# A graph network's edge loop: the VectorE instructions given one PSUM input each

## Chip, cores and metric

One NeuronCore of a Trainium2 chip runs the kernel. The metric is the device time of one execution, in microseconds (us); lower is better. The kernel is one launch and works in fp32 except for small 0/1 tables in bf16.

## The reference, cut to what matters

Four layers of message passing over 3125 nodes and 100000 edges with 64 channels. The edges arrive sorted by their target `dst`. Each layer does this, with `e` computed once:

```
msg = relu(h[src] + e) + 1e-7             # 100000 x 64
m = msg * t                               # t: one number per layer
seg_max = segment_max(m, dst)             # per node and channel
ex = exp(m - seg_max[dst])
agg = segment_sum(msg * ex, dst) / segment_sum(ex, dst)
out = h + agg
h' = relu(layernorm(out @ w1 + b1)) @ w2 + b2     # then residual and layernorm between layers
```

What takes the time is the part over edges: the gather `h[src]`, the maximum and the two sums per target.

## The kernel before, in words

**Tiles.** The 100000 edges are cut into two halves, one on partitions 0 to 63 and one on 64 to 127 (a partition is a channel of a half), and each half into 98 chunks of 512 edges. The edge loop therefore has 98 turns per layer and 392 in all; a turn works on tiles of 128 x 512 fp32. Layer 0 is written out (it also computes `e`, and counts the edges of each node); layers 1 to 3 are one loop body that runs three times.

**A turn `c`, engine by engine.** GpSimd (POOL in the rows) issues 8 indirect DMAs (L479). Each reads 128 row numbers from the SBUF table `idx_all` and fetches 128 rows of 64 values from `z_rows` in HBM into one of 7 buffers `zsrc`. GpSimd may run 7 turns ahead; it waits for `x_mm` of turn c-7. TensorE (PE) writes `pR` (a row of 0 or -1e30 that marks where a new target begins, L713), adds `e_in` and the gathered rows into `pX` (L722, L727), and transposes the results of the turn before into `pT` (L738, function `back`). ScalarE (ACT) makes `r = relu(pX)` (L556) and `du[1] = r * t` (L558), copies `pT` out (L568), and takes the exponential of the double tile `du`, 1024 elements wide (L562). VectorE (DVE) makes the running maximum `M` with a scan (L1011), `du[0] = pR + M shifted by one` (L1014), subtracts `M` from both halves of `du` in one instruction (L1016), forms `rex = r * ex[1]` (L1023), and scans the two running sums `S` and `W` (L1025, L1027). The sums decay by `exp(du[0])`, which is 0 at a new target, so the last edge of a target holds its sums. SyncE stores `M`, `S` and `W` to HBM and loads `e_in`.

**What sets the order.** Every engine's program is written by hand, with semaphores. `pX`, `pR` and `pT` have two PSUM banks each, used in turn; 8 banks are all there are. In layer 0 VectorE also builds `hot_hi` and `hot_lo` (L1033, L1035, function `node_one_hots`) in 80 of the 98 turns. They stand behind the two sums. After the 98 turns of a layer comes a tail: the last sums are stored, a seam between the halves is mended, 25 more indirect DMAs (L488) fetch each node's sums, and the small matrices and layer norms over nodes run. GpSimd issues no gather of the next layer before that is done.

The lines that the change touches are `messages` and `exps` on ScalarE, `falls` and `add_edges` on TensorE, and `running_max` and `running_sums` on VectorE:

Of the kernel before, what the change touches and what calls it, by code (L numbers as in the profile page):

```python
# [27 lines left out]
P = 128  # L28
# [25 lines left out]
PRE = 2  # L54
# [8 lines left out]
def program(nc, x, src, dst, attr, enc_w, enc_b, edge_w, edge_b, ln_g, ln_b, w1, b1, g1, bb1, w2, b2, t, out):  # L63
    ctx = ExitStack()
    with ctx:
# [64 lines left out]
        r = two("r", [P, CH])  # L130
        du = two("du", [P, 2, CH])
        ex = two("ex", [P, 2, CH])
        rex = sb("rex", [P, CH])
        M = two("M", [P, CH + 1])
# [116 lines left out]
        r_done = sem("r_done")  # L251
        u_done = sem("u_done")
        m_done = sem("m_done")
        d_done = sem("d_done")
        du_done = sem("du_done")
        ex_done = sem("ex_done")
        rex_done = sem("rex_done")
        sw_done = sem("sw_done")
# [239 lines left out]
        def _(act):  # L498
# [30 lines left out]
            act.sem_inc(r_done, PRE)  # L529
            act.sem_inc(u_done, PRE)  # L530
            act.sem_inc(ex_done, PRE)
            act.sem_inc(back_sb, 2 * PRE)
# [5 lines left out]
            def layer(l, first_layer=False):  # L538
# [13 lines left out]
                def messages(c):  # L552
                    s = c % 2
                    act.wait_ge(x_mm, done(g0 + c))
                    act.wait_ge(rex_done, done(g0 + (c - 2)))
                    act.activation(r[s][:, :], pX[s][:, :], ACT.Relu).then_inc(r_done, 1)  # L556
                    act.wait_ge(r_done, done(g0 + c))
                    act.activation(du[s][:, 1, :], r[s][:, :], ACT.Copy, scale=t_now[:, 0:1]).then_inc(u_done, 1)  # L558

                def exps(c):  # L560
                    act.wait_ge(du_done, done(g0 + c))
                    act.activation(ex[c % 2][:, :, :], du[c % 2][:, :, :], ACT.Exp).then_inc(ex_done, 1)  # L562

# [81 lines left out]
        def _(pe):  # L645
# [45 lines left out]
            def layer(l, first_layer=False):  # L691
# [18 lines left out]
                def falls(c):  # L710
                    pe.wait_ge(d_done, done(g0 + (c - 2)))
                    for h in range(2):
                        pe.matmul(pR[c % 2][h * H:(h + 1) * H, :], chunk_sel[:, c:c + 1].to_broadcast([NCH, H]), fall_sb[:, h, :],  # L713
                                  start=True, stop=True)

                def add_edges(c):
                    if first_layer:
                        pe.wait_ge(e_ready, c + 1)
                    else:
                        pe.wait_ge(e_loaded[c % RING], value(pe, (l - 1) * (16 * USES)) + 16 * (c // RING + 1))  # L720
                    pe.wait_ge(r_done, done(g0 + (c - 2)))
                    pe.matmul(pX[c % 2][:, :], ident[:, :], e_in[c % RING][:, :], start=True, stop=False, skip_group_check=True)  # L722
# [114 lines left out]
        def _(dve):  # L837
# [141 lines left out]
            dve.wait_ge(par_in, 16 * N_PAR)  # L979
            for counter in (m_done, d_done, du_done, rex_done, sw_done, agg_done, y_hat_done, hres_done):  # L980
                dve.sem_inc(counter, PRE)
# [10 lines left out]
            def layer(l, first_layer=False):  # L992
# [14 lines left out]
                def running_max(c):  # L1007
                    s, s1 = c % 2, (c - 1) % 2
                    dve.wait_ge(u_done, done(g0 + c))
                    dve.wait_ge(m_stored[s], q0 * 16 + (c // 2 + 1) * 16)  # L1010
                    v.tensor_tensor_scan(M[s][:, 1:CH + 1], pR[s][:, :], du[s][:, 1, :], M[s1][:, CH:CH + 1], ALU.add, ALU.max)  # L1011
                    v.tensor_copy(M[s][:, 0:1], M[s1][:, CH:CH + 1]).then_inc(m_done, 1)
                    dve.wait_ge(m_done, done(g0 + c))
                    v.tensor_tensor(du[s][:, 0, :], pR[s][:, :], M[s][:, 0:CH], ALU.add).then_inc(d_done, 1)  # L1014
                    dve.wait_ge(d_done, done(g0 + c))
                    v.tensor_tensor(du[s][:, :, :], du[s][:, :, :], M[s][:, None, 1:CH + 1].to_broadcast([P, 2, CH]),  # L1016
                                    ALU.subtract).then_inc(du_done, 1)

                def running_sums(c):
                    s, s1 = c % 2, (c - 1) % 2  # L1020
                    dve.wait_ge(ex_done, done(g0 + c))
                    dve.wait_ge(sw_done, done(g0 + (c - 1)))
                    v.tensor_tensor(rex[:, :], r[s][:, :], ex[s][:, 1, :], ALU.mult).then_inc(rex_done, 1)  # L1023
                    dve.wait_ge(back_tp, 2 * g0 + 2 * c + (2 * PRE - 2))
                    v.tensor_tensor_scan(S[s][:, :], ex[s][:, 0, :], ex[s][:, 1, :], S[s1][:, CH - 1:CH], ALU.mult, ALU.add)  # L1025
                    dve.wait_ge(rex_done, done(g0 + c))
                    v.tensor_tensor_scan(W[s][:, :], ex[s][:, 0, :], rex[:, :], W[s1][:, CH - 1:CH], ALU.mult, ALU.add).then_inc(sw_done, 1)  # L1027

# [53 lines left out]
                for c in range(NCH):  # L1082
                    running_max(c)
                    running_sums(c)
                    if first_layer and 0 <= c - HOT_AT < NHB:
                        node_one_hots(c - HOT_AT)
                    if first_layer and c - HOT_AT == NHB + 1:
                        node_ends_1()
# [112 lines left out]
```

## Time and profile before

| | |
|---|---|
| median of 3 runs | 4679.84 us (4676.88 to 4680.34) |
| the profiled execution's own time | 4680.27 us |
| its span, first to last instruction | 4678.2 us |
| GpSimd busy | 3372.7 us (72%) |
| VectorE busy | 2830.4 us (61%) |
| TensorE busy | 2485.0 us (53%) |
| ScalarE busy | 1559.0 us (33%) |
| granted TensorE clock, mean | 0.694 of full |

A busy time is the sum of an engine's instruction durations. GpSimd's spans are the time from taking up a gather to having issued it; the data land later. The gap between two gathers (about 0.30 us) is not counted as busy and is called "issue" in the rows: the engine waited for nothing that the profile shows.

### The profile page before, as it was taken

The numbers are of one execution on the slowest core, as the hardware profiler recorded it, in microseconds if no ns is written. First come the engines' busy times: TensorE is split into PE (matmuls) and PEld (weight loads), VectorE is DVE, ScalarE is ACT, GpSimd is POOL, SyncE is SP. The second block draws the span as 40 slices with busy tenths as digits, with TensorE's granted clock in tenths as the row PEclk, the third lists the DMA queues.
The fourth block names the chain that finished last, engine by engine and source line by source line (L and its number), as shares of the span: only waits on it lengthen the run. The fifth ranks groups of instructions, "written<-read, shape, count | busy, mean of one in ns | idle before, by whom it ended". The sixth has DMA issues, their size and how long they took to land.

```text
span 4678.2 us, 37695 instructions
## 1 busy us (share of the span) xinstructions
PE 2485.0 (53%) x9917; PEld 1798.9 (38%) x9917; DVE 2830.4 (61%) x3516; ACT 1559.0 (33%) x2689; POOL 3372.7 (72%) x3248
## 2 busy tenths in 40 slices
PE   4666666665455555555355555555544555555553
PEld 3444445443333333333233333333332333333333
DVE  5777777765565555555455555555555555555554
ACT  2444444443333333333233333333332333333333
POOL 4777777775577777777557777777746777777773
PEclk9887887877566666666656666666656666666665
DMA  3444444444144444444224444444423444444441
GB/s 87 129 132 130 131 135 128 132 128 127 51 112 112 112 112 112 112 112 112 79 69 113 110 112 111 112 112 111 114 56 89 111 111 112 111 111 111 111 112 48
DMA packets 419935, 506.67 MB, mean 108 GB/s; under 512 B 189115, under 2 KB 190247, under 8 KB 419700
## 3 DMA queue, kind: packets, MB, share of 16 engines
q1 hardware_dynamic: 308294, 393.85, 26.5%
q0 software_dynamic: 108352, 109.48, 12.7%
q8 instruction: 87, 1.43, 0.1%
q14 instruction: 148, 1.21, 0.1%
q10 hardware_dynamic: 3054, 0.71, 0.1%
HBM read 216.21 MB, written 287.39 MB: 108 GB/s over the span
## 4 chain that ended last, share of the span: by engine, by line
POOL 53%; issue 17%; DMA 2%; DVE 2%; PE 1%; ACT 0%; POOLq 0%; DVEq 0%; SPq 0%
POOL zsrc L479 51%; POOL node_sw L488 2%; DMA z_rows<-z 1%; DMA sw_rows<-seam_sw 0%; DMA node_sw<-sw_rows,row_idx 0%; PE pX L796 0%; DVE z L1150 0%; PE pR L817 0%; DVE rden L1121 0%; POOLq L475 0%; ACT sq L601 0%; DMA zsrc<-z_rows,idx_all 0%; PE pT L808 0%; DVE z L1153 0%; DMA seam_sw<-sw_rows 0%
## 5 line engine op out<-in xcount | busy, mean ns | idle before, releaser
L479 POOL DMA_INDIRECT zsrc<-z_rows,idx_all x3136 | 3249.8, 1036 | 1108.9 <-issue 1021.0
L727 PE MATMUL pX<-ident,zsrc 128*128 128x128 f32 x3136 | 790.1, 431 | 1914.7 <-DMA zsrc<-z_rows,idx_all 1914.7
L727 PEld LDWEIGHTS pX<-ident,zsrc 128*128 128x128 f32 x3136 | 675.5, 318 | 2288.6 <-DMA zsrc<-z_rows,idx_all 2287.5
L1011 DVE TENSOR_TENSOR_SCAN M<-pR,M,du 128x512 f32<-128x512 f32 x392 | 503.5, 1284 | 1167.3 <-ACT du L558 1167.3
L556 ACT ACTIVATE r<-pX 128x512 f32<-128x512 f32 x392 | 234.2, 598 | 1986.4 <-PE pX L727 1986.4
L562 ACT ACTIVATE ex<-du 128x1024 f32<-128x1024 f32 x392 | 414.0, 1056 | 777.3 <-DVE du L1016 776.6
L738 PE MATMUL pT<-ident,S 128*128 128x128 f32 x1568 | 638.5, 410 | 30.0 <-DVE W L1027 30.0
L738 PE MATMUL pT<-ident,W 128*128 128x128 f32 x1568 | 628.3, 404 | 0.0
L1023 DVE TENSOR_TENSOR rex<-r,ex 128x512 f32<-128x512 f32 x392 | 281.5, 718 | 440.7 <-ACT ex L562 440.7
L722 PE MATMUL pX<-e_in,ident 128*128 128x512 f32 x784 | 519.5, 749 | 7.5 <-ACT e_in L550 7.5
L1025 DVE TENSOR_TENSOR_SCAN S<-ex,S 128x512 f32<-128x512 f32 x392 | 499.1, 1273 | 0.0
L1027 DVE TENSOR_TENSOR_SCAN W<-ex,W,rex 128x512 f32<-128x512 f32 x392 | 492.0, 1255 | 0.0
L1016 DVE TENSOR_TENSOR du<-du,M 128x1024 f32<-128x1024 f32 x392 | 480.3, 1225 | 13.3
L568 ACT ACTIVATE sw_out<-pT 128x512 f32<-128x512 f32 x784 | 426.7, 586 | 29.4 <-PE pT L738 28.5
L738 PEld LDWEIGHTS pT<-ident,S 128*128 128x128 f32 x1568 | 358.5, 229 | 31.8 <-issue 23.2
L738 PEld LDWEIGHTS pT<-ident,W 128*128 128x128 f32 x1568 | 357.6, 228 | 0.0
L558 ACT ACTIVATE du<-r,t_now 128x512 f32<-128x512 f32 x392 | 283.0, 722 | 12.9
L1014 DVE TENSOR_TENSOR du<-pR,M 128x512 f32<-128x512 f32 x392 | 270.9, 691 | 13.5
L488 POOL DMA_INDIRECT node_sw<-sw_rows,row_idx x100 | 121.2, 1212 | 157.4 <-DMA sw_rows<-seam_sw 94.9
L713 PE MATMUL pR<-fall_sb,chunk_sel 98*64 98x512 bf16 x784 | 203.1, 515 | 15.6 <-DVEq L1171 15.6
L722 PEld LDWEIGHTS pX<-e_in,ident 128*128 128x128 f32 x784 | 145.1, 232 | 137.5 <-issue 106.8
L708 PE MATMUL pA<-attr_t,edge_w 128*128 128x512 f32 x196 | 125.0, 725 | 11.7 <-ACT attr_t L544 11.3
(155 smaller groups left out, 1406.5 us busy)
## 6 DMA issues: line engine op xcount, KB each, us to landing
sw_rows<-sw_out SPq DMA_DIRECT2D x784, 256.0 KB, 2.8
e_in<-e_cols SPq DMA_DIRECT2D x300, 256.0 KB, 2.7
zsrc<-z_rows,idx_all POOLq DMA_INDIRECT x3136
max_cols<-M SPq DMA_DIRECT2D x392, 128.0 KB, 2.3
attr_in<-in_edge_attr_dram SPq DMA_DIRECT2D x196, 128.0 KB
e_cols<-e_in SPq DMA_DIRECT2D x98, 256.0 KB, 2.1
z_rows<-z SPq DMA_DIRECT2D x5, 781.2 KB
node_sw<-sw_rows,row_idx POOLq DMA_INDIRECT x100, 3.3
```

The lines of the kernel that those rows point to most:

```text
L479: pool.indirect_dma_start(zsrc[c % RING][:, t4, h, :], None, z_rows, bass.IndirectOffsetOnAxis(idx_all[:, h, t4, c:c + 1].bitcast(U32), 0) ...
L558: act.activation(du[s][:, 1, :], r[s][:, :], ACT.Copy, scale=t_now[:, 0:1]).then_inc(u_done, 1)
L562: act.activation(ex[c % 2][:, :, :], du[c % 2][:, :, :], ACT.Exp).then_inc(ex_done, 1)
L568: act.activation(sw_out[c % 2][:, :, 2 * b:2 * b + 2, :, :].rearrange("p h t s c -> p (t s) h c"), pT[b][:, :].rearrange("p (a h c) -> p a ...
L722: pe.matmul(pX[c % 2][:, :], ident[:, :], e_in[c % RING][:, :], start=True, stop=False, skip_group_check=True)
L727: last = pe.matmul(pX[c % 2][:, t4:CH:SUB], zsrc[c % RING][:, t4, :, :].rearrange("p h c -> p (h c)"), ident[:, :], start=False, stop=(t4 ...
L738: last = pe.transpose(pT[b][:, at:at + P], scanned[c % 2][:, t4:CH:SUB], ident[:, :])
L1011: v.tensor_tensor_scan(M[s][:, 1:CH + 1], pR[s][:, :], du[s][:, 1, :], M[s1][:, CH:CH + 1], ALU.add, ALU.max)
L1016: v.tensor_tensor(du[s][:, :, :], du[s][:, :, :], M[s][:, None, 1:CH + 1].to_broadcast([P, 2, CH]), ALU.subtract).then_inc(du_done, 1)
L1023: v.tensor_tensor(rex[:, :], r[s][:, :], ex[s][:, 1, :], ALU.mult).then_inc(rex_done, 1)
L1025: v.tensor_tensor_scan(S[s][:, :], ex[s][:, 0, :], ex[s][:, 1, :], S[s1][:, CH - 1:CH], ALU.mult, ALU.add)
L1027: v.tensor_tensor_scan(W[s][:, :], ex[s][:, 0, :], rex[:, :], W[s1][:, CH - 1:CH], ALU.mult, ALU.add).then_inc(sw_done, 1)
```

## The change

Every two-tensor instruction of VectorE in the edge loop now takes one input from PSUM. For that:

- the double tiles `du` and `ex` and the tile `rex` are gone; `u` (r * t) and `decay` are single tiles in SBUF;
- ScalarE writes `r * t` twice, once to `u` in SBUF and once back into `pX` in PSUM;
- VectorE adds `M` to `pR` in place, subtracts `M` from `pR` in place and from `pX` in place: three instructions of 512 elements where there were one of 512 and one of 1024;
- ScalarE's exponential is two instructions of 512: `pR` to `decay`, and `pX` in place;
- `S` is scanned from `decay` and `pX`; then `r` is multiplied into `pX` in place, and `W` is scanned from `decay` and `pX`. The product now comes behind the scan of `S`;
- TensorE may write `pR` again when `decay` is done (was: when the first sum was), and `pX` when `W` is done (was: when `r` was);
- the copy of one column of `M` goes ahead of the scan; in layer 0 `node_one_hots` stands between the maximum and the sums.

```diff
-        du = two("du", [P, 2, CH])
-        ex = two("ex", [P, 2, CH])
-        rex = sb("rex", [P, CH])
+        u = two("u", [P, CH])
+        decay = two("decay", [P, CH])
...
-                    act.activation(du[s][:, 1, :], r[s][:, :], ACT.Copy, scale=t_now[:, 0:1]).then_inc(u_done, 1)
+                    act.activation(u[s][:, :], r[s][:, :], ACT.Copy, scale=t_now[:, 0:1]).then_inc(u_done, 1)
+                    act.activation(pX[s][:, :], r[s][:, :], ACT.Copy, scale=t_now[:, 0:1]).then_inc(u_ps_done, 1)
 
                 def exps(c):
-                    act.wait_ge(du_done, done(g0 + c))
-                    act.activation(ex[c % 2][:, :, :], du[c % 2][:, :, :], ACT.Exp).then_inc(ex_done, 1)
+                    act.wait_ge(dm_done, done(g0 + c))
+                    act.activation(decay[c % 2][:, :], pR[c % 2][:, :], ACT.Exp).then_inc(decay_done, 1)
+                    act.wait_ge(um_done, done(g0 + c))
+                    act.activation(pX[c % 2][:, :], pX[c % 2][:, :], ACT.Exp).then_inc(ex_done, 1)
...
                 def falls(c):
-                    pe.wait_ge(d_done, done(g0 + (c - 2)))
+                    pe.wait_ge(decay_done, done(g0 + (c - 2)))
...
-                    pe.wait_ge(r_done, done(g0 + (c - 2)))
+                    pe.wait_ge(sw_done, done(g0 + (c - 2)))
                     pe.matmul(pX[c % 2][:, :], ident[:, :], e_in[c % RING][:, :], start=True, stop=False, skip_group_check=True)
...
                     s, s1 = c % 2, (c - 1) % 2
+                    v.tensor_copy(M[s][:, 0:1], M[s1][:, CH:CH + 1])
                     dve.wait_ge(u_done, done(g0 + c))
                     dve.wait_ge(m_stored[s], q0 * 16 + (c // 2 + 1) * 16)
-                    v.tensor_tensor_scan(M[s][:, 1:CH + 1], pR[s][:, :], du[s][:, 1, :], M[s1][:, CH:CH + 1], ALU.add, ALU.max)
-                    v.tensor_copy(M[s][:, 0:1], M[s1][:, CH:CH + 1]).then_inc(m_done, 1)
+                    v.tensor_tensor_scan(M[s][:, 1:CH + 1], pR[s][:, :], u[s][:, :], M[s1][:, CH:CH + 1], ALU.add, ALU.max).then_inc(m_done, 1)
                     dve.wait_ge(m_done, done(g0 + c))
-                    v.tensor_tensor(du[s][:, 0, :], pR[s][:, :], M[s][:, 0:CH], ALU.add).then_inc(d_done, 1)
+                    v.tensor_tensor(pR[s][:, :], pR[s][:, :], M[s][:, 0:CH], ALU.add).then_inc(d_done, 1)
                     dve.wait_ge(d_done, done(g0 + c))
-                    v.tensor_tensor(du[s][:, :, :], du[s][:, :, :], M[s][:, None, 1:CH + 1].to_broadcast([P, 2, CH]),
-                                    ALU.subtract).then_inc(du_done, 1)
+                    v.tensor_tensor(pR[s][:, :], pR[s][:, :], M[s][:, 1:CH + 1], ALU.subtract).then_inc(dm_done, 1)
+                    dve.wait_ge(u_ps_done, done(g0 + c))
+                    v.tensor_tensor(pX[s][:, :], pX[s][:, :], M[s][:, 1:CH + 1], ALU.subtract).then_inc(um_done, 1)
 
                 def running_sums(c):
                     s, s1 = c % 2, (c - 1) % 2
+                    dve.wait_ge(decay_done, done(g0 + c))
                     dve.wait_ge(ex_done, done(g0 + c))
                     dve.wait_ge(sw_done, done(g0 + (c - 1)))
-                    v.tensor_tensor(rex[:, :], r[s][:, :], ex[s][:, 1, :], ALU.mult).then_inc(rex_done, 1)
                     dve.wait_ge(back_tp, 2 * g0 + 2 * c + (2 * PRE - 2))
-                    v.tensor_tensor_scan(S[s][:, :], ex[s][:, 0, :], ex[s][:, 1, :], S[s1][:, CH - 1:CH], ALU.mult, ALU.add)
+                    v.tensor_tensor_scan(S[s][:, :], decay[s][:, :], pX[s][:, :], S[s1][:, CH - 1:CH], ALU.mult, ALU.add).then_inc(s_done, 1)
+                    dve.wait_ge(s_done, done(g0 + c))
+                    v.tensor_tensor(pX[s][:, :], r[s][:, :], pX[s][:, :], ALU.mult).then_inc(rex_done, 1)
                     dve.wait_ge(rex_done, done(g0 + c))
-                    v.tensor_tensor_scan(W[s][:, :], ex[s][:, 0, :], rex[:, :], W[s1][:, CH - 1:CH], ALU.mult, ALU.add).then_inc(sw_done, 1)
+                    v.tensor_tensor_scan(W[s][:, :], decay[s][:, :], pX[s][:, :], W[s1][:, CH - 1:CH], ALU.mult, ALU.add).then_inc(sw_done, 1)
...
                 for c in range(NCH):
                     running_max(c)
-                    running_sums(c)
                     if first_layer and 0 <= c - HOT_AT < NHB:
                         node_one_hots(c - HOT_AT)
+                    running_sums(c)
```

VectorE in layer 0, one turn of the stretch with one-hots, before (digits are the buffer of a pair; a scan is listed as SCALAR_TENSOR_TENSOR):

```order
L1011 SCALAR_TENSOR_TENSOR M0<-pR0,M1,du0 128x512 [waits m_stored0,u_done]
L1012 COPY M0<-M1 128x1
L1014 TENSOR_TENSOR du0<-pR0,M0 128x512 [waits m_done]
L1016 TENSOR_TENSOR du0<-du0,M0 128x1024 [waits d_done]
L1023 TENSOR_TENSOR rex<-r0,ex0 128x512 [waits sw_done,ex_done]
L1025 SCALAR_TENSOR_TENSOR S0<-ex0,S1 128x512 [waits back_tp]
L1027 SCALAR_TENSOR_TENSOR W0<-ex0,W1,rex 128x512 [waits rex_done]
L1033 TENSOR_TENSOR hot_hi0<-count_b,hi_b 125x1250 [waits hot_used]
L1035 TENSOR_TENSOR hot_lo0<-count_b,lo_b 125x250
```

and with the change (line numbers are those of the changed kernel):

```order
L1017 COPY M0<-M1 128x1
L1020 SCALAR_TENSOR_TENSOR M0<-pR0,M1,u0 128x512 [waits m_stored0,u_done]
L1022 TENSOR_TENSOR pR0<-pR0,M0 128x512 [waits m_done]
L1024 TENSOR_TENSOR pR0<-pR0,M0 128x512 [waits d_done]
L1026 TENSOR_TENSOR pX0<-pX0,M0 128x512 [waits u_ps_done]
L1044 TENSOR_TENSOR hot_hi0<-count_b,hi_b 125x1250 [waits hot_used]
L1046 TENSOR_TENSOR hot_lo0<-count_b,lo_b 125x250
L1034 SCALAR_TENSOR_TENSOR S0<-decay0,S1,pX0 128x512 [waits sw_done,back_tp,ex_done,decay_done]
L1036 TENSOR_TENSOR pX0<-r0,pX0 128x512 [waits s_done]
L1038 SCALAR_TENSOR_TENSOR W0<-decay0,W1,pX0 128x512 [waits rex_done]
```

The one-hots moved from behind `W` to between the last subtraction and `S`, the product from before `S` to behind it, and one more instruction is issued per turn.

ScalarE in the loop of layers 1 to 3, one turn, before:

```order
L556 ACTIVATE r0<-pX0 128x512 [waits rex_done,x_mm]
L558 ACTIVATE du0<-r0,t_now 128x512 [waits r_done]
L567 REGISTER_ALU [waits sw_stored1]
L568 ACTIVATE sw_out1<-pT0 128x4x2x64 [waits back_tp]
L567 REGISTER_ALU
L568 ACTIVATE sw_out1<-pT1 128x4x2x64 [waits back_tp]
L562 ACTIVATE ex0<-du0 128x1024 [waits du_done]
```

and with the change:

```order
L561 ACTIVATE r0<-pX0 128x512 [waits rex_done,x_mm]
L563 ACTIVATE u0<-r0,t_now 128x512 [waits r_done]
L564 ACTIVATE pX0<-r0,t_now 128x512
L575 REGISTER_ALU [waits sw_stored1]
L576 ACTIVATE sw_out1<-pT0 128x4x2x64 [waits back_tp]
L575 REGISTER_ALU
L576 ACTIVATE sw_out1<-pT1 128x4x2x64 [waits back_tp]
L568 ACTIVATE decay0<-pR0 128x512 [waits dm_done]
L570 ACTIVATE pX0<-pX0 128x512 [waits um_done]
```

Two more instructions per turn: the second `r * t`, ahead of the copies out, and the exponential in two pieces.

## Rows read from the trace of the kernel before

**Rows 1.** The page, the chain that ended last: shares by engine, then by line.

```profile
POOL 53%; issue 17%; DMA 2%; DVE 2%; PE 1%; ACT 0%; POOLq 0%; DVEq 0%; SPq 0%
```

**Rows 2.** GpSimd's gathers: duration in ns, least, median and greatest.

```profile
L479 POOL DMA_INDIRECT zsrc<-z_rows,idx_all x3136: 940/944/2181, 58.8 to 4569.5; - x196
```

**Rows 3.** Busy time of the gathers alone, by stretch: layers 0, 1, 2, 3.

```profile
58.00:1143.00 1085.00, 844.64 (x784) 0.80 0.47 129
1244.00:2282.00 1038.00, 798.35 (x784) 0.68 0.41 111
2384.00:3424.00 1040.00, 800.98 (x784) 0.67 0.40 110
3526.00:4571.00 1045.00, 805.03 (x784) 0.67 0.40 110
```

**Rows 4.** Timeline in layer 2, VectorE and GpSimd: start, duration, instruction, idle before.

```profile
2803.29 1.28 DVE L1011 TENSOR_TENSOR_SCAN M<-pR,M,du 128x512 f32<-128x512 f32 x1 [2.97 <-ACT du L558]
...
2803.95 0.94 POOL L479 DMA_INDIRECT zsrc<-z_rows,idx_all  x1 [0.30 <-issue]
...
2804.65 0.69 DVE L1014 TENSOR_TENSOR du<-pR,M 128x512 f32<-128x512 f32 x1
...
2808.37 1.27 DVE L1025 TENSOR_TENSOR_SCAN S<-ex,S 128x512 f32<-128x512 f32 x1
2808.98 1.42 POOL L479 DMA_INDIRECT zsrc<-z_rows,idx_all  x1 [0.30 <-issue]
2809.57 1.25 DVE L1027 TENSOR_TENSOR_SCAN W<-ex,W,rex 128x512 f32<-128x512 f32 x1
...
2810.70 0.94 POOL L479 DMA_INDIRECT zsrc<-z_rows,idx_all  x1 [0.30 <-issue]
```

**Rows 5.** Timeline in layer 0, the 1024-element subtraction and the one-hots beside gathers.

```profile
701.95 1.45 DVE L1033 TENSOR_TENSOR hot_hi<-count_b,hi_b 125x1250 bf16<-125x1250 bf16 x1
...
703.16 1.06 POOL L479 DMA_INDIRECT zsrc<-z_rows,idx_all  x1 [0.30 <-issue]
703.33 0.41 DVE L1035 TENSOR_TENSOR hot_lo<-count_b,lo_b 125x250 bf16<-125x250 bf16 x1
...
705.47 1.28 DVE L1011 TENSOR_TENSOR_SCAN M<-pR,M,du 128x512 f32<-128x512 f32 x1 [1.73 <-ACT du L558]
...
718.68 1.22 DVE L1016 TENSOR_TENSOR du<-du,M 128x1024 f32<-128x1024 f32 x1
...
719.23 1.49 POOL L479 DMA_INDIRECT zsrc<-z_rows,idx_all  x1 [0.30 <-issue]
```

**Rows 6.** The page's costliest groups: count, busy us, mean ns, idle before and its releaser.

```profile
L479 POOL DMA_INDIRECT zsrc<-z_rows,idx_all x3136 | 3249.8, 1036 | 1108.9 <-issue 1021.0
L727 PE MATMUL pX<-ident,zsrc 128*128 128x128 f32 x3136 | 790.1, 431 | 1914.7 <-DMA zsrc<-z_rows,idx_all 1914.7
...
L1011 DVE TENSOR_TENSOR_SCAN M<-pR,M,du 128x512 f32<-128x512 f32 x392 | 503.5, 1284 | 1167.3 <-ACT du L558 1167.3
L556 ACT ACTIVATE r<-pX 128x512 f32<-128x512 f32 x392 | 234.2, 598 | 1986.4 <-PE pX L727 1986.4
L562 ACT ACTIVATE ex<-du 128x1024 f32<-128x1024 f32 x392 | 414.0, 1056 | 777.3 <-DVE du L1016 776.6
...
L1023 DVE TENSOR_TENSOR rex<-r,ex 128x512 f32<-128x512 f32 x392 | 281.5, 718 | 440.7 <-ACT ex L562 440.7
...
L1016 DVE TENSOR_TENSOR du<-du,M 128x1024 f32<-128x1024 f32 x392 | 480.3, 1225 | 13.3
L568 ACT ACTIVATE sw_out<-pT 128x512 f32<-128x512 f32 x784 | 426.7, 586 | 29.4 <-PE pT L738 28.5
...
L558 ACT ACTIVATE du<-r,t_now 128x512 f32<-128x512 f32 x392 | 283.0, 722 | 12.9
L1014 DVE TENSOR_TENSOR du<-pR,M 128x512 f32<-128x512 f32 x392 | 270.9, 691 | 13.5
```

More of the change, by code:

```diff
@@ L252, in program @@
         u_done = sem("u_done")
+        u_ps_done = sem("u_ps_done")
         m_done = sem("m_done")
         d_done = sem("d_done")
-        du_done = sem("du_done")
+        dm_done = sem("dm_done")
+        um_done = sem("um_done")
+        decay_done = sem("decay_done")
         ex_done = sem("ex_done")
+        s_done = sem("s_done")
         rex_done = sem("rex_done")
@@ L530, in _ @@
             act.sem_inc(u_done, PRE)
+            act.sem_inc(u_ps_done, PRE)
+            act.sem_inc(decay_done, PRE)
             act.sem_inc(ex_done, PRE)
@@ L979, in _ @@
             dve.wait_ge(par_in, 16 * N_PAR)
-            for counter in (m_done, d_done, du_done, rex_done, sw_done, agg_done, y_hat_done, hres_done):
+            for counter in (m_done, d_done, dm_done, um_done, s_done, rex_done, sw_done, agg_done, y_hat_done, hres_done):
                 dve.sem_inc(counter, PRE)
```

## The prediction

> **What bounds the kernel now.** I read the chain of waits first. More than half of the span on it is GpSimd, and 17% is "issue", the pauses between its gathers [rows 1]. The groups say what the rest does meanwhile: TensorE waits 1914.7 us for gathered rows, ScalarE 1986.4 us for TensorE, VectorE 1167.3 us for ScalarE [rows 6]. So inside the edge loop everybody waits for the gathers, and GpSimd waits for nobody: each gather follows the last after 0.30 us [rows 4]. A turn of the loop costs 8 gathers.
>
> Then I asked whether a gather always takes the same time. It does not. The median is 944 ns and the least 940, but the mean is 1036 and the greatest 2181 [rows 2, 6]. Most gathers sit at the floor, and some are held up. What the long ones have in common is seen in the timeline, by laying GpSimd's rows beside VectorE's:
> - A gather that starts 0.66 us into the scan of M takes 0.94 us. That scan reads pR in PSUM and du in SBUF [rows 4].
> - A gather that starts 0.61 us into the scan of S takes 1.42 us. That scan reads two tiles in SBUF. The gather's remaining 0.94 us begin at 2809.46, 0.18 us before the scan is over at 2809.64 [rows 4].
> - A gather that starts 0.55 us into the 1024-element subtraction, again two inputs in SBUF, takes 1.49 us. Its last 0.94 us begin at 719.78, 0.12 us before the end at 719.90 [rows 5].
> - A gather at 703.16 beside hot_hi, also two inputs in SBUF, takes 1.06 us, and its last 0.94 us begin 0.12 us before the end of hot_hi [rows 5].
> - A gather that starts 1.13 us into the scan of W, when under 0.12 us of it is left, takes 0.94 us [rows 4].
>
> So a gather that wants to start while VectorE runs an instruction with two SBUF inputs waits until about 0.12 to 0.18 us before its end, and one with a PSUM input holds up nothing. The gather reads its row numbers from SBUF (idx_all), which is why I take it to be a matter of reading SBUF.
>
> **How much is lost to it.** Per layer the busy time of the 784 gathers less 784 x 0.944 us (740.1 us) is 104.5 us in layer 0, and 58.3, 60.9 and 64.9 us in layers 1 to 3 [rows 2, 3]. The sum is 288.6 us, all of it on the path. This is the most that the change can give by this route.
>
> **The change, part by part.**
>
> *Layers 1 to 3.* Subtraction, product and both scans all get a PSUM input, so no two-input SBUF instruction is left in the loop. The 184.1 us go.
>
> *Layer 0.* The same goes for its loop, but hot_hi and hot_lo still read two SBUF tiles, 80 times. Now each costs 0.12 us at 703.16 [rows 5], some 10 us in all. That is luck of phase: a gather starts 1.21 us into it. With the one-hots moved, they fall elsewhere against the gathers. hot_hi holds gathers up for 1.45 - 0.12 = 1.33 us and a gather starts every 0.944 + 0.30 = 1.244 us, so one always falls inside it. It waits nothing at best and 1.33 us at worst; over evenly spread phases the mean is 1.33 x 1.33 / 2 / 1.244 = 0.71 us. hot_lo adds 0.29 x 0.29 / 2 / 1.244 = 0.03 us. I take the mean, since in layer 0 the landings jitter: 80 x 0.74 = 60 us stay. Bounds 0 and 106 us.
>
> *Longer or shorter VectorE.* Its turn now runs from the start of the M scan to the end of W, 2803.29 to 2810.82, 7.53 us [rows 4]. Afterwards: M scan 1.28 and 0.04 to the next; addition 0.69 + 0.04; first subtraction 0.69; second 0.69, less 0.06 overlap; then it waits for the second exponential, 0.60 with two hand-overs of 0.03; scan S 1.28 + 0.04; product 0.69 + 0.04; scan W 1.28. Sum 7.36 us. The prices: 691 ns for 512 elements with PSUM in and SBUF out, 1284 for a scan with one PSUM input, 598 for an activation of 512 [rows 6]. No row shows VectorE or ScalarE writing PSUM, or an instruction that reads and writes the same bank; the lower bound is the same 691, since nothing there leaves out work. The upper bound is 1225 ns, the row of twice the elements, as if the bank served read and write in turn; for the exponential 1056 in place of 598 [rows 6]. I take the low ends: same element count, same input. With the high ends the turn is 7.36 + 4 x 0.53 + 0.46 = 9.94 us. GpSimd's is 8 x 1.244 = 9.95 us. So even there VectorE only draws level.
>
> *ScalarE* gets one r * t more (722 ns) and one start-up more in the exponential (2 x 598 - 1056 = 140 ns): 0.598 + 2 x 0.722 + 2 x 0.586 + 2 x 0.598 = 4.4 us of a turn of 9.95 [rows 6]. Zero; hidden under the wait for TensorE. The second r * t ends while VectorE is in its M scan, so nobody waits for it. Layer 0 adds two activations of about that size and still has room.
>
> *The two later releases.* TensorE may write pX of turn c+1 only when W of turn c-1 is done. But its program puts the transposes of turn c-1 right ahead, and those wait for the same W. Nothing is queued longer. The same holds for pR and decay. Zero.
>
> *The one-hots ahead of the sums* fill the wait for the exponentials (440.7 us over 392 turns now, 1.12 each [rows 6]). VectorE in layer 0 needs 7.36 - 0.66 + 1.39 + 0.41 = 8.5 us of a turn of about 10.7. Zero.
>
> *Gathers, loads, stores, the tails between layers* are the same instructions in the same order. The time from the last gather to the last sum changes by about 0.2 us in four tails. Zero.
>
> **The sum.** 4680.3 us of the profiled execution (the median of the runs is 4679.8, the same within 0.01%), less 288.6, plus 60: **4452 us**. With the bounds for hot_hi, 4392 to 4498.
>
> **Rivals.**
>
> *A: only the input's place matters, and the wrong one stays.* In the row that shows no hold-up, PSUM is the first input. In the new S, product and W it is the second. If a first input from SBUF holds gathers as well, the subtraction's part goes but the scan's 0.48 us per turn stays [rows 4]: 392 x 0.48 = 188 us. 4452 + 188 = 4640 us. For it: no row has this operand order. Against: both orders need one SBUF read. Chance 0.05.
>
> *B: the hold-up is not VectorE's reading.* Then nothing changes but phases: 4680 us, within a few us. By what mechanism: a gather must write what it issues, and two-input instructions would then not be what stops it. Against it: the end of the wait follows the end of three different instructions with two SBUF inputs within 0.12 to 0.18 us, and never that of the M scan. Chance 0.03. The Trainium skill, "SBUF — State Buffer", section "Who interferes with whom", speaks for B in part: it says that `tensor_tensor` did not stall such DMAs in a probe, and infers that it takes only the shared read interface while the issuing of descriptors needs the write interface. By that the sum would be 4680. The same section also says that two SBUF inputs contend with a GpSimd instruction that reads SBUF. The trace agrees with this second rule and not with the first: 1.49 us beside a `tensor_tensor` [rows 5].
>
> *C: VectorE becomes the bound, slower than before.* The place is the in-place instructions on pR and pX. One turn now takes 1038 / 98 = 10.6 us in layers 1 to 3 [rows 3]. With the exponential at its 1.06 us, VectorE's turn passes 10.6 us if each of the four in-place ones takes over (10.6 - 7.36 - 0.46) / 4 + 0.69 = 1.39 us. That is the point from which it decides. If they cost three times per element (0.16 + 3 x 0.53 = 1.76 us, from 691 and 1225), and the exponential 1.51, the turn is 7.36 + 4.28 + 0.91 = 12.6 us: +2.0 x 294 in layers 1 to 3, and about +1.7 x 80 in layer 0, some 5400 us. For it: no row covers such an instruction. Against: it must be worse than doubled. Chance 0.03.
>
> *D: between.* Doubled prices put VectorE level with GpSimd; then every jitter of a landing is paid by both and the turn is some 0.1 to 0.2 us longer than 9.95: 4452 + 392 x 0.15 = 4510 us. Chance 0.07.
>
> **The numbers.** My forecast has 0.82, A 0.05, B 0.03, C 0.03, D 0.07. A measurement of this kernel tells 0.2% (9 us) from no change. Faster: forecast, A and D, 0.94. Same: B, 0.03. Slower: C, 0.03. The range takes in the forecast's bounds, 4392 to 4498, trimmed at the bottom because no hold-up at all is an unlikely phase, and D at the top: 4400 to 4525.
>
> **What would show it.** The gathers' mean falls from 1036 to about 963 ns (944 + 60 us / 3136), with a median of 944 again. In layers 1 to 3 the 784 gathers take 740 us busy and the stretch 975 instead of 1038. In layer 0 about 800 us, every long gather beside hot_hi or hot_lo. The in-place instructions read 0.69 us, scans 1.28. TensorE still waits for zsrc. The forecast is wrong if gathers of 1.4 us stand beside the new scans (A), if the mean stays at 1036 (B), or if gaps of over 0.30 us appear between gathers in mid-loop because x_mm is late (C, D).

## The result, and the profile after

The changed kernel takes 4442.67 us (median of 4 runs, 4438.64 to 4442.86), the kernel before 4678.36 us. The ratio is 0.9492, 95% interval 0.9481 to 0.9504: **faster by 5.1%**, 236 us. The forecast was 4452 us, in a range of 4400 to 4525. Left out of all that follows are one of the four executions of hot_psum (5396.28 us, the other three 4390.20 to 4391.09) and the first runs of pad_psum3 and hot_psum_behind, beside which the kernel before took 5231.89 us instead of some 4678.

The gathers of the changed kernel, by instruction (duration in ns: least, median, greatest) and by stretch, layers 0 to 3 (busy time of the gathers alone):

```profile
L482 POOL DMA_INDIRECT zsrc<-z_rows,idx_all x3136: 940/944/2232, 58.6 to 4332.1; - x196
```
```profile
58.00:1093.00 1035.00, 792.17 (x784) 0.83 0.48 136
1192.00:2172.00 980.00, 739.94 (x784) 0.68 0.43 117
2273.00:3253.00 980.00, 739.96 (x784) 0.69 0.43 117
3353.00:4334.00 981.00, 740.00 (x784) 0.69 0.43 117
```

Compare [rows 2] and [rows 3]. The least and the median have not moved (940, 944), but in layers 1 to 3 the 784 gathers of a layer now take 740 us, which is 784 x 0.944: none is held up by more than 0.04 us. Layer 0 went from 844.6 to 792.2 us and keeps 52 us above 784 x 0.944.

The page's chain of waits and its groups, the counterparts of [rows 1] and [rows 6]:

```profile
POOL 52%; issue 18%; DMA 2%; DVE 2%; PE 1%; ACT 0%; POOLq 0%; DVEq 0%; SPq 0%
```
```profile
L482 POOL DMA_INDIRECT zsrc<-z_rows,idx_all x3136 | 3012.1, 960 | 1108.4 <-issue 1019.8
L735 PE MATMUL pX<-ident,zsrc 128*128 128x128 f32 x3136 | 772.8, 424 | 1649.7 <-DMA zsrc<-z_rows,idx_all 1649.7
...
L1020 DVE TENSOR_TENSOR_SCAN M<-pR,M,u 128x512 f32<-128x512 f32 x392 | 503.2, 1284 | 1001.2 <-ACT u L563 1000.8
...
L1034 DVE TENSOR_TENSOR_SCAN S<-decay,S,pX 128x512 f32<-128x512 f32 x392 | 500.9, 1278 | 253.2 <-ACT decay L568 240.0
...
L1038 DVE TENSOR_TENSOR_SCAN W<-decay,W,pX 128x512 f32<-128x512 f32 x392 | 501.8, 1280 | 13.8
...
L1022 DVE TENSOR_TENSOR pR<-pR,M 128x512 f32<-128x512 f32 x392 | 274.2, 699 | 13.6
L1024 DVE TENSOR_TENSOR pR<-pR,M 128x512 f32<-128x512 f32 x392 | 274.1, 699 | 13.5
L1036 DVE TENSOR_TENSOR pX<-r,pX 128x512 f32<-128x512 f32 x392 | 272.7, 696 | 13.5
L1026 DVE TENSOR_TENSOR pX<-pX,M 128x512 f32<-128x512 f32 x392 | 269.9, 688 | 0.0
L564 ACT ACTIVATE pX<-r,t_now 128x512 f32<-128x512 f32 x392 | 263.2, 671 | 0.0
...
L570 ACT ACTIVATE pX<-pX 128x512 f32<-128x512 f32 x392 | 228.8, 584 | 0.2
```

The gathers' busy time fell by 3249.8 - 3012.1 = 237.7 us, and the span by 4678.2 - 4441.0 = 237.2 us. That is the whole effect: VectorE is busier than before (2918.6 us against 2830.4), ScalarE too (1819.6 against 1559.0), and both still wait for the gathers. In-place work in PSUM costs what the same shape cost with an SBUF output: 688 to 699 ns against 691; the activations that write PSUM are even a little shorter (671 and 584 ns against 722 for `u` and 595 for `decay`, L563 and L568).

The timeline of one turn in layer 2, VectorE and GpSimd (start, duration, instruction, idle before), the counterpart of [rows 4]:

```profile
2798.42 1.28 DVE L1020 TENSOR_TENSOR_SCAN M<-pR,M,u 128x512 f32<-128x512 f32 x1 [2.76 <-ACT u L563]
...
2802.56 1.28 DVE L1034 TENSOR_TENSOR_SCAN S<-decay,S,pX 128x512 f32<-128x512 f32 x1 [0.79 <-ACT decay L568]
2803.28 0.94 POOL L482 DMA_INDIRECT zsrc<-z_rows,idx_all  x1 [0.30 <-issue]
...
2804.60 1.28 DVE L1038 TENSOR_TENSOR_SCAN W<-decay,W,pX 128x512 f32<-128x512 f32 x1
```

A gather that starts 0.72 us into the scan of S takes 0.94 us, where one at 0.61 us took 1.42 before. Over the whole trace 246 gathers start inside the scan of S (its last 0.21 us aside) and none is held; before the change 302 did, and all 302 were held. VectorE's turn is 2798.42 to 2805.88, 7.46 us. And in layer 0, the one-hots, the counterpart of [rows 5]:

```profile
701.94 1.45 DVE L1044 TENSOR_TENSOR hot_hi<-count_b,hi_b 125x1250 bf16<-125x1250 bf16 x1
...
702.42 1.79 POOL L482 DMA_INDIRECT zsrc<-z_rows,idx_all  x1 [0.30 <-issue]
```

This gather starts 0.48 us into hot_hi and waits 0.85 us, where the one at 703.16 waited 0.12. Of the 52 us left in layer 0, the waits beside hot_hi are 50.7.

### The profile page after: what moved, and what is told of

Same layout as the page of the kernel before. It is cut to its first block, busy times and chain, and to the rows that moved or that the text cites. A ratio compares the mean times of both kernels' runs of the same rounds, so it can differ in the third digit from the quotient of the medians.

```text
span 4441.0 us, 38976 instructions
## 1 busy us (share of the span) xinstructions
PE 2474.3 (56%) x9917; PEld 1760.4 (40%) x9917; DVE 2918.6 (66%) x3908; ACT 1819.6 (41%) x3473; POOL 3135.1 (71%) x3248
## 4 chain that ended last, share of the span: by engine, by line
POOL 52%; issue 18%; DMA 2%; DVE 2%; PE 1%; ACT 0%; POOLq 0%; DVEq 0%; SPq 0%
POOL zsrc L482 50%; POOL node_sw L491 2%; DMA z_rows<-z 1%; DMA sw_rows<-seam_sw 1%; DMA node_sw<-sw_rows,row_idx 0%; PE pX L804 0%; DVE z L1161 0%; DVE rden L1132 0%; PE pR L825 0%; POOLq L478 0%; PE pT L816 0%; ACT sq L609 0%; DMA zsrc<-z_rows,idx_all 0%; DMA seam_sw<-sw_rows 0%; DVE z L1164 0%
## 5 line engine op out<-in xcount | busy, mean ns | idle before, releaser
L482 POOL DMA_INDIRECT zsrc<-z_rows,idx_all x3136 | 3012.1, 960 | 1108.4 <-issue 1019.8
L1020 DVE TENSOR_TENSOR_SCAN M<-pR,M,u 128x512 f32<-128x512 f32 x392 | 503.2, 1284 | 1001.2 <-ACT u L563 1000.8
L1034 DVE TENSOR_TENSOR_SCAN S<-decay,S,pX 128x512 f32<-128x512 f32 x392 | 500.9, 1278 | 253.2 <-ACT decay L568 240.0
L746 PE MATMUL pT<-ident,S 128*128 128x128 f32 x1568 | 629.5, 405 | 51.7 <-DVE W L1038 51.5
L1038 DVE TENSOR_TENSOR_SCAN W<-decay,W,pX 128x512 f32<-128x512 f32 x392 | 501.8, 1280 | 13.8
L568 ACT ACTIVATE decay<-pR 128x512 f32<-128x512 f32 x392 | 233.3, 595 | 379.0 <-DVE pR L1024 379.0
L563 ACT ACTIVATE u<-r,t_now 128x512 f32<-128x512 f32 x392 | 283.0, 722 | 12.9
L1022 DVE TENSOR_TENSOR pR<-pR,M 128x512 f32<-128x512 f32 x392 | 274.2, 699 | 13.6
L1024 DVE TENSOR_TENSOR pR<-pR,M 128x512 f32<-128x512 f32 x392 | 274.1, 699 | 13.5
L1036 DVE TENSOR_TENSOR pX<-r,pX 128x512 f32<-128x512 f32 x392 | 272.7, 696 | 13.5
L1026 DVE TENSOR_TENSOR pX<-pX,M 128x512 f32<-128x512 f32 x392 | 269.9, 688 | 0.0
L564 ACT ACTIVATE pX<-r,t_now 128x512 f32<-128x512 f32 x392 | 263.2, 671 | 0.0
```

Of the source, the lines that this page charges most:

```text
L482: pool.indirect_dma_start(zsrc[c % RING][:, t4, h, :], None, z_rows, bass.IndirectOffsetOnAxis(idx_all[:, h, t4, c:c + 1].bitcast(U32), 0) ...
L563: act.activation(u[s][:, :], r[s][:, :], ACT.Copy, scale=t_now[:, 0:1]).then_inc(u_done, 1)
L746: last = pe.transpose(pT[b][:, at:at + P], scanned[c % 2][:, t4:CH:SUB], ident[:, :])
L1020: v.tensor_tensor_scan(M[s][:, 1:CH + 1], pR[s][:, :], u[s][:, :], M[s1][:, CH:CH + 1], ALU.add, ALU.max).then_inc(m_done, 1)
L1022: v.tensor_tensor(pR[s][:, :], pR[s][:, :], M[s][:, 0:CH], ALU.add).then_inc(d_done, 1)
L1024: v.tensor_tensor(pR[s][:, :], pR[s][:, :], M[s][:, 1:CH + 1], ALU.subtract).then_inc(dm_done, 1)
```

## The experiments

Two theories were open after the result. *The first:* a gather is held up by VectorE's second read from SBUF, wherever it comes from, and GpSimd sets the pace, so the time is a constant plus the held time (what the gathers take beyond 0.944 us each). *The second:* something else about the rewritten loop gave the gain: other lengths, other waits, other phases, or a write. Every edit is made to the changed kernel. The kernel before ran beside each (medians 4676 to 4681 us). A run has 2 to 8 executions, within 10 us of each other. Where the text says how many gathers were held, or sums the waits beside one instruction, that is counted over the whole trace: a wait belongs to the VectorE instruction near whose end it ended.

### A delay of the scan, and the same delay with its input in SBUF

```diff
+        exs = two("exs", [P, CH])
...
+                    act.activation(exs[c % 2][:, :], pX[c % 2][:, :], ACT.Exp)
                     act.activation(pX[c % 2][:, :], pX[c % 2][:, :], ACT.Exp).then_inc(ex_done, 1)
```

> The changed kernel, with one more ScalarE instruction per turn: the exponential of pX is also written to an SBUF tile exs (nobody reads it), ahead of the one in place. S starts some 0.6 us later per turn. It is the control of s_sbuf_late. Theory (a gather is held up only by a VectorE instruction with two SBUF inputs; GpSimd sets the pace): no gather is held in layers 1 to 3, VectorE's turn grows from 7.4 to about 8.0 us of 9.98, time 4443 us within 10. Rival (VectorE's or ScalarE's chain is near to being the bound, so that a delay of 0.6 us per turn shows): 4443 + 392 x 0.6 = 4680 us.

Measured: 4441.65 us. The scan of S waits 1.30 us for the exponentials where it waited 0.79, and that costs nothing; the rival's 4680 is out. Now the same instructions, one operand changed:

```diff
-                    v.tensor_tensor_scan(S[s][:, :], decay[s][:, :], pX[s][:, :], S[s1][:, CH - 1:CH], ALU.mult, ALU.add).then_inc(s_done, 1)
+                    v.tensor_tensor_scan(S[s][:, :], decay[s][:, :], exs[s][:, :], S[s1][:, CH - 1:CH], ALU.mult, ALU.add).then_inc(s_done, 1)
```

> As s_psum_late, instruction for instruction, but the scan of S reads exs in SBUF in place of pX in PSUM, so it has two SBUF inputs. Same values. Theory: each gather that starts in the first 1.1 us of that scan waits until about 0.18 us before its end. By the phases of the changed kernel's timeline, shifted by 0.6 us, the wait is 0.7 to 1.0 us per turn in layers 1 to 3 and 0.5 on average in layer 0: 4443 + 205 to 290 + 47 = 4695 to 4780 us. Rival (the hold-up was not VectorE's second SBUF read but the write side or something else about the old loop): 4443 us, as the control.

Measured: 4553.96 us, 112 us more than the control. In the control 376 gathers start inside the scan of S (its last 0.21 us aside) and none is held; here 298 do and 278 are held, and 19 of the 20 others start in its first 0.1 us. So the mechanism is right and the size was missed: I had expected 250 to 340. The timeline (layer 2, start and duration) shows one reason. One turn has a held gather, the next has none:

```profile
2799.97 1.28 DVE L1036 TENSOR_TENSOR_SCAN S<-decay,S,exs 128x512 f32<-128x512 f32 x1 [1.30 <-issue]
2800.55 1.46 POOL L483 DMA_INDIRECT zsrc<-z_rows,idx_all  x1 [0.31 <-issue]
...
2809.80 0.94 POOL L483 DMA_INDIRECT zsrc<-z_rows,idx_all  x1 [0.30 <-issue]
2809.90 1.28 DVE L1036 TENSOR_TENSOR_SCAN S<-decay,S,exs 128x512 f32<-128x512 f32 x1 [1.30 <-issue]
2811.05 0.94 POOL L483 DMA_INDIRECT zsrc<-z_rows,idx_all  x1 [0.30 <-issue]
```

The second scan falls between two starts: one gather starts 0.10 us ahead of it and is free, the next 1.15 us into it and is free again. What a gather needs to be let in for is its start. The hold is 1.1 us, the gathers' distance 1.25, so a scan can slip through; I had taken one timeline's phase for all turns. In layers 1 to 3 a gather is held in 60 to 65 of a layer's 98 turns, and its wait is 0.45 us on average, where I had 0.7 to 1.0 us in every turn.

### One part undone: the subtraction in SBUF

```diff
-                    v.tensor_tensor(pR[s][:, :], pR[s][:, :], M[s][:, 1:CH + 1], ALU.subtract).then_inc(dm_done, 1)
-                    dve.wait_ge(u_ps_done, done(g0 + c))
-                    v.tensor_tensor(pX[s][:, :], pX[s][:, :], M[s][:, 1:CH + 1], ALU.subtract).then_inc(um_done, 1)
+                    v.tensor_tensor(du[s][:, :, :], du[s][:, :, :], M[s][:, None, 1:CH + 1].to_broadcast([P, 2, CH]),
+                                    ALU.subtract).then_inc(dm_done, 1)
...
```

The cut lines are what this needs: ScalarE writes `r * t` once, to `du`, the addition writes to `du`, and the exponentials read `du`.

> The changed kernel with the subtraction as it was: one instruction of 1024 elements with two SBUF inputs (du, M); the exponentials then go to decay in SBUF and to pX in PSUM, and product and scans stay as changed. Same values. It is the change without one of its parts. Theory: gathers are held only beside this instruction. Its hold is 1.1 us; by the phases of the changed kernel's timeline a gather starts 0.3 to 0.7 us into it, so it waits 0.4 to 0.8 us per turn: 4443 + 130 to 235 in layers 1 to 3 + about 48 in layer 0 = 4620 to 4725 us. So undoing one of four parts may give back nearly the whole gain. Rival (the parts add up: in the kernel before this instruction held gathers for 88 us by its own rows): 4530 us.

Measured: 4585.66 us, 143 us above the changed kernel. That is below my interval, which started at 4620, and above the rival's 4530. The gathers' groups say 3155.0 us busy, 143 us over the changed kernel's. Beside the subtraction the gathers wait 174.8 us, where they waited 86.8 us beside the same instruction in the kernel before. In layer 0 part of it was taken back: hot_hi's waits became short again, 18.8 us in all against 50.7 in the changed kernel. Undoing one part of four loses 60% of the gain, so the parts do not add up: what an instruction costs depends on where the others have left the gathers.

### A useless instruction of three kinds

All three stand between the product and the scan of W and have about the same length. The first, with one input from PSUM:

```diff
+                    v.tensor_tensor(pad_o[:, :, :], pX[s][:, None, :].to_broadcast([P, 2, CH]), pad_b[:, None, :].to_broadcast([P, 2, CH]), ALU.add)
```

> The changed kernel with one useless VectorE addition of 1024 elements per turn between the product and the scan of W, its inputs pX (PSUM) and a constant tile in SBUF. Theory: it takes 1.22 us, VectorE's turn grows to 8.6 us in layers 1 to 3, GpSimd still sets the pace and no gather is held by it: 4443 us within 10. Rival (VectorE's length matters): 4443 + 392 x 1.2 = 4910 us.

Measured: 4439.34 us. 1224 ns more of VectorE per turn cost nothing. A gather beside it, in layer 2:

```profile
2799.69 1.22 DVE L1044 TENSOR_TENSOR pad_o<-pX,pad_b 128x1024 f32<-128x1024 f32 x1
2799.99 0.94 POOL L485 DMA_INDIRECT zsrc<-z_rows,idx_all  x1 [0.30 <-issue]
```

With `pad_a`, in SBUF, in place of `pX[s]`:

> As pad_psum, but both inputs of the useless addition are constant tiles in SBUF. Same length, same place. Theory: a gather that starts in its first 1.1 us waits until 0.12 us before its end; in the changed kernel gathers start 0.1 to 0.4 us behind that point in most turns, so 0.7 to 1.0 us of waiting in most turns: 4443 + 200 to 300 + about 48 = 4690 to 4790 us. Rival (it is not the two SBUF inputs): 4443 us as pad_psum.

Measured: 4664.97 us, 226 us more than with the PSUM input; nearly the whole gain of the change is gone. That is a little under the expectation, for the reason above: in layers 1 to 3 the addition holds a gather in 70 to 75 of 98 turns. The row that does it, in layer 2, with a gather that starts at the same 0.30 us into the addition:

```profile
2807.60 1.22 DVE L1044 TENSOR_TENSOR pad_o<-pad_a,pad_b 128x1024 f32<-128x1024 f32 x1
2807.90 1.75 POOL L485 DMA_INDIRECT zsrc<-z_rows,idx_all  x1 [0.30 <-issue]
```

The last 0.94 us of that gather begin at 2808.71, 0.11 us before the end of the addition. With the PSUM input 361 gathers start inside the addition (its last 0.21 us aside) and none is held; with both inputs in SBUF 301 do and 286 are held, and the 15 others start in its first 0.05 us.

The third is a copy of 2048 elements, SBUF to SBUF, one input:

```diff
+                    v.tensor_copy(pad_o[:, :, :], pad_a[:, :, :])
```

> As pad_sbuf, but the useless instruction is a VectorE copy of 2048 fp32 elements from SBUF to SBUF, one input. Theory of the second read alone: one input, nothing is held, 4443 us. Rival (a copy from SBUF to SBUF holds the gathers too, as if it were reading through both ports): it then takes about 1.2 us and costs as pad_sbuf, 4690 to 4790 us.

Measured: 4743.74 us, more than the kernel before (4675.74). So the theory that only a second tensor matters is wrong, and the rival is right: a copy with one input holds gathers too. It moves 2048 elements in 1.23 us, where the addition needs 1.22 us for 1024. Its rows (layer 2) show a second kind of hold:

```profile
2701.75 0.94 POOL L484 DMA_INDIRECT zsrc<-z_rows,idx_all  x1 [0.30 <-issue]
2702.28 1.46 DVE L1042 COPY pad_o<-pad_a 128x2048 f32<-128x2048 f32 x1
2703.00 1.55 POOL L484 DMA_INDIRECT zsrc<-z_rows,idx_all  x1 [0.30 <-issue]
...
2712.34 1.65 POOL L484 DMA_INDIRECT zsrc<-z_rows,idx_all  x1 [0.30 <-issue]
2712.64 1.23 DVE L1042 COPY pad_o<-pad_a 128x2048 f32<-128x2048 f32 x1
```

The gather at 2712.34 started 0.30 us before the copy and was held all the same: it ends at 2713.99, 0.12 us after the copy's end. In the whole traces neither the scan of s_sbuf_late nor the addition of pad_sbuf holds a gather that has started before it; the copy holds every one that started up to 0.51 us before it. And at 2702.28 it is the copy that is held, 1.46 us in place of 1.23, and it came 0.53 us into a gather; the copies that come 0.51 to 0.74 us into one take 1.48 down to 1.25 us. From this I take it that a gather wants something not only at its start but again in its middle, and that the copy excludes that too; what it is, no run shows.

The Trainium skill, "SBUF — State Buffer", section "Who interferes with whom", has these pieces: an exclusive lock on ports that VectorE and GpSimd share, taken by copies in a two-port mode for reading and writing, and by two SBUF inputs for reading only, the later of the two to wait. The trace agrees in that copies and two-input instructions are the ones that hold gathers, and with 1.46 us for a copy that came second. The section also says that whichever starts first has the ports for its whole instruction; there the trace differs, since the gather at 2712.34 started first and was held. Its remark that `tensor_tensor` did not stall such DMAs does not hold for these indirect ones: 210 us of waits beside the addition here.

### How far VectorE can grow

The addition of pad_psum three times per turn.

> As pad_psum, with three such additions of 1024 elements per turn (pX in PSUM and a constant tile in SBUF, each into its own tile). It looks for the point at which VectorE becomes the bound. Theory: VectorE's turn is 7.4 + 3 x 1.2 = 11.0 us in layers 1 to 3 and about 12.1 in layer 0, against 9.98 and 10.5 of GpSimd now. So VectorE sets the pace: 4443 + 1.0 x 294 + 1.6 x 98 = 4890 us, within 40, and gaps of over 0.30 us stand between gathers in mid-loop. Rival (the slack is larger, because part of the chain overlaps with the next turn's gathers): 4443 us.

Measured: 5438.03 us, left out as said with the result. The same kernel again:

> The kernel of pad_psum3 once more. In that run the kernel before took 5232 us beside it instead of 4680, so it says nothing about pace. Same expectation: VectorE's turn is 11.0 us in layers 1 to 3 and 12.1 in layer 0, and sets the pace: 4890 us within 40. Rival (the slack is larger): 4443 us.

Measured: 4856.31 us, within 40 of the 4890 expected. The groups:

```profile
L484 POOL DMA_INDIRECT zsrc<-z_rows,idx_all x3136 | 3028.7, 966 | 1224.9 <-issue 1001.4
L748 PE MATMUL pT<-ident,S 128*128 128x128 f32 x1568 | 676.6, 432 | 1929.3 <-DVE W L1045 1929.3
```

TensorE now waits for W, 1929.3 us, and hardly for the gathers (78.1 us). The timeline has the scan of S at 2002.55 and again at 2013.36, so the turn is 10.81 us, all of it VectorE's but 0.8 for the exponentials. In the changed kernel eight gathers take 8 x (0.944 + 0.304) = 9.98 us and VectorE's turn 7.46, which leaves an estimated 2.5 us of room per turn. One addition of 1.2 fits and three do not; two were not tried.

### The one-hots: their place, and their input

Back behind the sums, nothing else:

> The changed kernel with the one-hots of layer 0 back behind the two sums; nothing else. Theory: hot_hi and hot_lo still hold gathers up, only at another phase; the sum of their waits is anywhere between 10 us (as before the change) and 106 us (80 x 1.33), so the time is 4400 to 4500 us, and layers 1 to 3 don't change. Rival (the place ahead of the sums matters because it covers the wait for the exponentials): VectorE's turn in layer 0 grows by 0.7 us to 9.2, still under 9.98, so this rival needs layer 0 to get longer with VectorE having no idle time left in a turn: 4443 + 80 x 0.7 = 4500 us.

Measured: 4428.84 us, 14 us faster than the changed kernel. The gathers' busy time is 3003.9 against 3012.1 us, so 8 of the 14 us are held time; the rest lies mostly in the tails between the layers. The place that the change gave them is not the better one.

Where they stand in the changed kernel, with the table of counts in unused columns of the PSUM bank `pH`:

```diff
+            v.tensor_copy(pH[0:NP, 256:256 + NP], count_i[:, :])
+            dve.drain()
...
-                    if n >= 2:
-                        dve.wait_ge(hot_used, n - 1)
+                    if n >= 1:
+                        dve.wait_ge(hot_used, n)
...
-                    v.tensor_tensor(hot_hi[n % 2][:, :, :], count_b[:, None, 0:NP].to_broadcast([NP, HB, NP]),
+                    v.tensor_tensor(hot_hi[n % 2][:, :, :], pH[0:NP, None, 256:256 + NP].to_broadcast([NP, HB, NP]),
...
-                    v.tensor_tensor(hot_lo[n % 2][:, :, :], count_b[:, None, 0:NK].to_broadcast([NP, HB, NK]),
+                    v.tensor_tensor(hot_lo[n % 2][:, :, :], pH[0:NP, None, 256:256 + NK].to_broadcast([NP, HB, NK]),
```

> The changed kernel, and the table of counts that both one-hots compare with is read from 125 fp32 columns of the PSUM bank pH instead of from SBUF; the one-hot of turn n waits until the counting matmuls of n-1, which write that bank, are done. Theory: the last held gathers go, 51 us in layer 0, which leaves 4390 to 4400 us. Risk: the new wait pushes VectorE's turn in layer 0 towards 9.8 us and eats some of it (up to 20 us). Rival (only fp32 tiles of the loop matter, or the mixture of a fp32 PSUM and a bf16 SBUF input still holds gathers): 4443 us.

Measured: **4390.79 us, ratio to the kernel before 0.9379 (0.9360 to 0.9398)**, 52 us faster than the changed kernel: the version that beats both. Its gathers, and a gather that starts 0.80 us into hot_hi, in layer 0:

```profile
L482 POOL DMA_INDIRECT zsrc<-z_rows,idx_all x3136 | 2961.7, 944 | 1108.9 <-issue 1020.5
```
```profile
110.54 1.45 DVE L1046 TENSOR_TENSOR hot_hi<-pH,hi_b 125x1250 bf16<-125x1250 f32 x1
111.34 0.94 POOL L482 DMA_INDIRECT zsrc<-z_rows,idx_all  x1 [0.30 <-issue]
```

The mean is the median, 944 ns. In all 80 turns a gather starts inside hot_hi, anywhere from 0.02 to 1.24 us into it, and none is held; in the changed kernel all 80 are. Both changes to the one-hots together:

> As hot_psum, with the one-hots behind the two sums. Theory: with no gather held by the one-hots their place is worth nothing, 4390 us as hot_psum, within 5. Rival (the place in itself, the cover of the wait for the exponentials or the wait for the counting matmuls, is worth something): it differs from hot_psum by 15 us or more, as hot_behind differs from the changed kernel by 14.

Measured: 5358.32 us, left out for the same reason. The same kernel again:

> The kernel of hot_psum_behind once more, for the same reason. Theory: 4390 us within 5, as hot_psum. Rival (the place of the one-hots in itself is worth something): 15 us or more away from it.

Measured: 4390.51 us. With nothing held, the place is worth nothing. So the 8 us of held time in hot_behind came from where the gathers happened to fall; its other 5 us are not explained.

### All runs on one line

Held time is the gathers' busy time less 3136 x 0.944 = 2960.4 us.

| kernel | span, us | held, us | span less held |
|---|---|---|---|
| before | 4678.2 | 289.4 | 4388.8 |
| changed | 4441.0 | 51.7 | 4389.3 |
| s_psum_late | 4440.7 | 53.5 | 4387.2 |
| s_sbuf_late | 4550.1 | 162.8 | 4387.3 |
| sub_sbuf | 4582.4 | 194.6 | 4387.8 |
| pad_psum | 4437.2 | 48.1 | 4389.1 |
| pad_sbuf | 4662.9 | 269.7 | 4393.2 |
| pad_copy | 4741.8 | 352.1 | 4389.7 |
| hot_behind | 4427.6 | 43.5 | 4384.1 |
| hot_psum | 4388.7 | 1.3 | 4387.4 |
| hot_psum_behind2 | 4387.9 | 1.5 | 4386.4 |

Eleven kernels with held times from 1 to 352 us leave the same 4384 to 4393 us. Only pad_psum3_again leaves the line (4854.2 - 68.3 = 4785.9), because there VectorE sets the pace. So the time is a constant plus the held time, as the first theory has it, and other lengths, waits and places are worth at most some 5 us by themselves, which is against the second. That it is the place of an operand which holds a gather is shown by the two pairs that differ in one operand, s_psum_late with s_sbuf_late and pad_psum with pad_sbuf. The first theory is too narrow in one point: pad_copy's copy has one input and holds gathers as well.

## Why the prediction was right

- **The bound and its loss.** Right. 288.6 us were called the most that could be had by this route; hot_psum gains 4678.2 - 4388.7 = 289.5. In the kernel before, the waits beside the scan of S sum to 145.0 us, beside the subtraction to 86.8, beside the product to 39.5 and beside hot_hi to 17.1.
- **Layers 1 to 3: 184.1 us go.** They went: 740 us of gathers in each. A layer's gathers span 979 us (784 x 1.248) and not the 975 forecast, because the pause between two is 0.304 us and not 0.300; the sum did not use the 975.
- **Layer 0: 60 us stay, bounds 0 and 106.** 52 us stayed, almost all of it beside hot_hi. This term is 8 of the 9 us between forecast and measurement. The waits beside hot_hi run from 0.12 to 1.29 us with a mean of 0.63, against the 0.71 of evenly spread phases, so the assumption holds in this kernel. That the number came so close is in part luck: the same 80 instructions cost 17.1 us in the kernel before (the prediction had some 10), 18.8 in sub_sbuf, 41.2 in hot_behind and 68.0 in pad_psum3_again. My expectations for s_sbuf_late and sub_sbuf, built on one turn's phase, were too high.
- **VectorE's turn, 7.36 us.** Measured 7.46. The unknown price, in-place work in PSUM, came out at the low end (688 to 699 ns), so rivals C and D had no footing. pad_psum3_again shows what C would have looked like: TensorE waits for W.
- **ScalarE, later releases, tails at zero.** Right: s_psum_late starts the scan of S 0.5 us later per turn and costs nothing.
- **Rival A**, a first input from SBUF: refuted by the changed kernel itself, whose S, product and W have that order. Its price was too high as well: it took a hold of 0.48 us in every turn, 188 us, and the scan of S cost 145.0. **Rival B**, not the reading: refuted by s_sbuf_late against s_psum_late, one operand apart.
- **Left open.** That it is the reading of idx_all which a gather needs at its start was argued from the code. No run moves the row numbers, so it is not shown. Nor is it tried whether smaller pieces of VectorE work would let gathers in earlier.

## What to carry to other kernels

When an engine that issues indirect DMAs sets the pace, compare the mean of its instruction with the median; a gap is time lost to something else, and laying VectorE's rows beside the long ones names it. Give each long two-input VectorE instruction one PSUM input where a bank is free, and keep large SBUF-to-SBUF copies away from such a stretch. Extra length on VectorE was free here for one addition of 1.2 us in a turn of 10 us, and no longer for three. Remove the last such instruction before judging an order: while some remain, phases decide, and a change that leaves one of four undone can return less than half of the gain (93 of 236 us here).

## What the runs showed of the hardware that I had not expected

A VectorE copy of 2048 fp32 elements from SBUF to SBUF (1.23 us) holds a gather even when that gather has started up to 0.51 us before it, and then the gather ends 0.12 us after the copy; one that started a little earlier, from 0.51 us on, holds the copy instead (1.48 us). Instructions with two SBUF inputs keep gathers from starting, until 0.11 to 0.13 us (scans: 0.17 to 0.20 us) before their end, and leave those that have started alone. A gather that starts just as they do, within about 0.05 us (scan: 0.1), goes free, and in pad_sbuf the addition then takes up to 1.30 us instead of 1.22. And an instruction that reads and writes the same PSUM bank element by element ran at the speed of one with an SBUF output.
